# A language-model tower: routing with unrolled loops, 64-column blocks and filler passes, and a table with picks in pairs

## The chip, the cores and the metric

One core of a Trainium2 chip runs the kernel. The metric is the device time of one execution in microseconds (us), the median of several runs; before the change it is 1200.1 us (three runs, 1199.15 to 1202.99). Engines: TensorE (PE; its weight loads PEld), VectorE (DVE), ScalarE (ACT), GpSimd (POOL) and SyncE (SP), each with its own stream of instructions, ordered between engines by semaphores alone.

## The reference

64 batches of 128 tokens, width 192. Three steps, each added to the residual h:

```
h = layernorm(concat(word_emb[x] + pos_emb, three graph features) @ W_proj.T + b_proj)
h = h + (causal long convolution per channel of layernorm(h)) + bias * layernorm(h)
x = layernorm(h)
top2, idx = top_k(x @ Wr.T, 2)           # 8 experts
w = softmax(top2)
h = h + sum over the two picks of w * (gelu(x @ Wi[e].T + bi[e]) @ Wo[e].T + bo[e])
```

The expert step computes only the picked experts: tokens are sorted by expert into tiles of 256 slots.

## The kernel before

The stages follow one another in time on the one core.

*Tokens* (0 to 491 us): gathers, graph features, projection and normalisation, in rounds of one quad (Q = 4 batches of 128 rows). *Convolution* (491 to 539 us): fp32 matmuls of 128 columns (L614), the results added to `Hs` by VectorE.

*Routing* (539 to 625 us), the stage that most of the change touches. Sixteen quads, in four groups g of four (GRP = 16 batches). For quad i, with p = i mod 2:

- VectorE: statistics of the rows of a group (L1032) and from these scale and shift (`scales`, L1034: a chain of small instructions). Before the first quad it does those of quads 0 and 1, 2 and 3, and group 1; those of groups 2 and 3 follow between the rankings of groups 0 and 1 (`groups`, L1089).
- ScalarE, `row_parts` (L826): four instructions (L830) write the normalised rows to `xn[p]`, fp32, 192 wide; one more (L834) rounds them to bf16 into the row table `xrow` (`hi`).
- GpSimd, `low` (L482): copies the last 64 columns of each row side by side into `xn1` (L486), waits for `hi_done`, and subtracts the rounded from the full values (L489, L490), the `lo` part.
- TensorE, `turn_quad` (L628): four transposes of the first 128 columns into bank 1 (L633), two of `xn1` into bank 2 (L635). It waits for `ln_done`, `xn1_ready` and `xnT_ready`.
- ScalarE, `turned_parts` (L836): two copies from PSUM to `xnT0` and `xnT1` (L839, L840).
- TensorE, `score` (L638): the fp32 product with the router's weights, six matmuls, which run as two passes each, of 16 columns (L643) and 8 (L645), into one of the four banks 3 to 6; it waits until the quad four back has been ranked (`gap_ready`).
- VectorE, `choices` (L1042): the two largest of eight scores and their places (L1047 to L1051).
- A group behind, the softmax of two (`gap_exp`, `shares`) and the one-hot counts (`rank`, L648: two bf16 products).

TensorE's order is: transposes of quad i+1, scores of quad i (`routes`, L659). ScalarE's: rows of quad i+1, copies of quad i. `steps` (L79) runs the first and the last rounds written out and those between in a loop of the engine. SyncE stores `Hs` and `xrow` by groups (`store_rows`, L401) once a group's weights are there, then loads the first experts' weights (L428, L431).

*Table* (625 to 670 us): VectorE turns counts into slots (L1116 to L1144). Then TG = 16 steps, double-buffered: VectorE compares slot numbers with a ramp, 142 values by eight picks for `hot_q` and 128 by eight for `hot_p` (`one_hot`, L1147); ScalarE scales `hot_q` into `hot_s`, four picks an instruction (L872); TensorE sums eight products `hot_p` x `hot_s`, each of 142 columns, in banks 5 and 6 (L680). The picks are innermost, so that the matmul of pick i reads both operands at a step of eight bf16 values, 16 bytes. Behind step 1 VectorE works out the expert of each tile (`experts`, L1151).

*Identifiers* (670 to 680 us): small VectorE instructions, then gathers of the first rows by GpSimd (L501), transposes by TensorE (L694). *Experts* (680 us to the end): 71 tiles, TensorE nearly throughout.

## Time and profile before

| what | value |
|---|---|
| median of three runs | 1200.1 us |
| profiled execution | 1199.93 us, span of its instructions 1198.0 us |
| mean granted clock of TensorE | 0.784 of 2.4 GHz |
| busy: TensorE / VectorE / ScalarE / GpSimd | 955.7 / 615.1 / 518.6 / 670.7 us |

The busy share of TensorE is 80%, but it is a mean over stages with different limits, and it counts a matmul at 1.2 GHz for twice what it would take at 2.4. So the page is read by stage: windows of the trace give each engine's busy time and the granted clock in a stretch, the timeline gives the distance from start to start of the same instruction in neighbouring quads or steps, which is what a quad or step costs. The times of engines other than TensorE don't hang on the granted clock.

### The profile page before, as it was taken

How to read it: one execution, taken by the hardware profiler on the slowest of the kernel's cores; microseconds unless marked ns; L12 is line 12 of the kernel's file. 1: busy time of each engine (PE TensorE's matmuls, PEld its weight loads, DVE VectorE, ACT ScalarE, POOL GpSimd, SP SyncE). 2: the span in 40 equal slices, each digit the busy share in tenths (PEclk: the TensorE clock that was granted, in tenths of full speed). 3: DMA queues.
4: the chain of work that ended last, by engine and by line, in shares of the span. 5: the costliest groups of instructions: out<-in, count | busy, mean ns of one | idle time of the engine just before them, and what ended most of it. 6: DMA issues, size and time to landing. Idle time of an engine off the chain costs nothing. (4 is left out here: it accounts for less than half of the span.)

```text
span 1198.0 us, 22895 instructions
## 1 busy us (share of the span) xinstructions
PE 955.7 (80%) x7666; PEld 907.0 (76%) x7666; DVE 615.1 (51%) x2089; ACT 518.6 (43%) x1211; POOL 670.7 (56%) x592
## 2 busy tenths in 40 slices
PE   1678677768677687594977699999988998999991
PEld 0578677778677687594964399999978998999981
DVE  2035343445444456538957356665544654665551
ACT  1002121311212123355755376767655665767660
POOL 6455564646565640003520268867767777888774
PEclk9975665656665666795555599999999999999996
DMA  6315261616162533581098174485486465434342
GB/s 208 106 53 176 81 209 53 217 50 214 46 222 94 170 110 114 167 241 53 1 256 263 28 199 62 61 224 129 86 218 151 60 141 120 61 61 61 61 51 30
DMA packets 101114, 146.96 MB, mean 123 GB/s; under 512 B 13476, under 2 KB 81223, under 8 KB 98983
## 3 DMA queue, kind: packets, MB, share of 16 engines
q0 software_dynamic: 39552, 53.26, 23.0%
q1 hardware_dynamic: 60470, 82.26, 21.8%
q10 hardware_dynamic: 1008, 10.34, 2.4%
q8 instruction: 50, 0.82, 0.3%
q14 instruction: 34, 0.27, 0.1%
HBM read 107.00 MB, written 38.82 MB: 122 GB/s over the span
## 5 line engine op out<-in xcount | busy, mean ns | idle before, releaser
L883 ACT ACTIVATE Hs<-bank,U 128x256 bf16<-128x256 f32 x426 | 212.4, 498 | 182.6 <-PE bank L715 153.8
L474 POOL DMA_INDIRECT ev_g<-in_word_emb,ids_i x192 | 192.9, 1004 | 166.1 <-PE bank L573 111.9
L510 POOL DMA_INDIRECT out<-Hs,id_s x142 | 236.6, 1666 | 85.4 <-issue 83.3
L1204 DVE TENSOR_TENSOR Hs<-Hs 128x512 bf16<-128x512 f32 x213 | 147.5, 692 | 146.6 <-ACT Hs L884 131.3
L884 ACT ACTIVATE Hs<-bank,U 128x256 f32<-128x256 f32 x426 | 214.6, 504 | 0.0
L730 PE MATMUL bank<-U,Hs 128*128 128x192 bf16 x852 | 211.6, 248 | 0.2 <-issue 0.2
L732 PE MATMUL bank<-U,Hs 128*128 128x192 bf16 x852 | 209.9, 246 | 0.0
L731 PE MATMUL bank<-U,Hs 128*128 128x192 bf16 x852 | 209.7, 246 | 0.0
L501 POOL DMA_INDIRECT blob<-xtab_d,id_g x142 | 144.2, 1015 | 111.7 <-DVEq L1188 61.1
L573 PE MATMUL bank<-cs,ev_g 128*128 128x1 f32 x384 | 97.8, 318 | 42.6 <-issue 42.6
L572 PE MATMUL bank<-cs,ev_g 128*128 128x1 f32 x384 | 96.1, 314 | 39.4 <-issue 39.3
L572 PEld LDWEIGHTS bank<-cs,ev_g 128*128 128x128 f32 x384 | 93.4, 293 | 39.7 <-issue 39.5
L573 PEld LDWEIGHTS bank<-cs,ev_g 128*128 128x128 f32 x384 | 94.8, 298 | 37.5 <-issue 37.5
L711 PE MATMUL bank<-blob,U 128*128 128x256 bf16 x426 | 116.7, 274 | 2.1 <-DVE blob L1193 2.1
L712 PE MATMUL bank<-blob,U 128*128 128x256 bf16 x426 | 116.6, 274 | 0.0
L713 PE MATMUL bank<-blob,U 128*128 128x256 bf16 x426 | 116.6, 274 | 0.0
L714 PE MATMUL bank<-blob,U 128*128 128x256 bf16 x426 | 116.6, 274 | 0.0
L715 PE MATMUL bank<-blob,U 128*128 128x256 bf16 x426 | 116.6, 274 | 0.0
L731 PEld LDWEIGHTS bank<-U,Hs 128*128 128x128 bf16 x852 | 84.2, 99 | 0.1
L730 PEld LDWEIGHTS bank<-U,Hs 128*128 128x128 bf16 x852 | 83.2, 98 | 0.5 <-issue 0.4
L732 PEld LDWEIGHTS bank<-U,Hs 128*128 128x128 bf16 x852 | 83.0, 97 | 0.1
L469 POOL DMA_INDIRECT emb_g<-in_word_emb,ids_i x64 | 61.7, 963 | 26.7 <-issue 18.6
(183 smaller groups left out, 1735.2 us busy)
## 6 DMA issues: line engine op xcount, KB each, us to landing
U<-blob_d SPq DMA_DIRECT2D x20, 771.0 KB
U<-blob_d SPq DMA_DIRECT2D x20, 672.0 KB
adj_s<-in_adj SPq DMA_DIRECT2D x48, 256.0 KB
ev_g<-kpad_d SPq DMA_DIRECT2D x24, 512.0 KB, 5.3
wst<-in_wsrc SPq DMA_DIRECT2D x8, 1344.0 KB
blob_d<-blob ACTq DMA_DIRECT2D x7, 1443.0 KB
xtab_d<-U SPq DMA_DIRECT2D x4, 1552.0 KB, 8.8
out<-Hs SPq DMA_DIRECT2D x4, 1536.0 KB, 11.5
```

Source lines behind the costliest of these rows:

```text
L474: pool.indirect_dma_start(ev_g[:, p, j, b, :], None, t["word_emb"], bass.IndirectOffsetOnAxis(ap=ids_i[:, 1 + j, i * Q + b:i * Q + b + 1], ...
L501: pool.indirect_dma_start(xg_f[:, q % RX, h, :], None, xtab_d, bass.IndirectOffsetOnAxis(ap=id_g[:, 2 * q + h:2 * q + h + 1], axis=0)).the ...
L510: pool.indirect_dma_start(out, bass.IndirectOffsetOnAxis(ap=id_s[:, 2 * q + h:2 * q + h + 1], axis=0), yo[:, q % RX, h, :], None, compute_ ...
L572: mm(bank[3][:, k:k + 1], ev_g[:, p, j, b, 0:D0], cs[:, p, k:k + 1], start=True, stop=True)
L573: last = mm(bank[3][:, 16 + k:17 + k], ev_g[:, p, j, b, D - 128:D], cs[:, p, k:k + 1], start=True, stop=True)
L711: mm(ps, hi[:, a], x0, start=True, stop=False)
L730: mm(ps, hh[w][:, f, n], hi[:, c], start=f == 0, stop=False)
L731: mm(ps, hh[w][:, f, n], lo[:, c], start=False, stop=False)
L732: last = mm(ps, hl[w][:, f, n], hi[:, c], start=False, stop=f == FC - 1)
L883: f(hh[w][:, d, :], ps, ACT.Gelu, bias=bi[:, d:d + 1])
L884: last = f(hf[w][:, d, :], ps, ACT.Gelu, bias=bi[:, d:d + 1])
L1204: last = v.tensor_tensor(hl[w][:, c:c + 2, :], hf[w][:, c:c + 2, :], hh[w][:, c:c + 2, :], ALU.subtract)
```

## The change

- Routing: the loops of TensorE, ScalarE, VectorE and GpSimd are written out.
- The normalised rows go into three blocks of 64 columns, each block with the quad's four batches side by side (`xn[p, r, b, d]`). A transpose takes two neighbouring batches of one block; so `xn1` and its copy are gone. The router's weights lie block-diagonal for every block (`wr`, loaded by two DMAs instead of three), and all twelve score passes have 16 columns. Scores go to three banks (LB = 3) instead of four.
- The bf16 rounding of a quad is done by GpSimd, ahead of its subtractions, instead of by ScalarE.
- TensorE gets filler passes, bf16 matmuls of 256 columns whose result nobody reads: 56 ahead of the first transposes, 3 behind each quad's transposes, 4 behind each quad's scores, 45 ahead of the table and 40 behind it.
- Table: the tiles have two picks innermost, `[a, m, n, i]` with i of 2, so that a matmul reads at a step of two values, 4 bytes. `iota_r` shrinks with it, and ScalarE's two instructions a step read and write without gaps.

```diff
@@ -36,6 +36,9 @@
 TG = 16
 TB = B // TG
 PICKS = 2 * TB
+XR = D // D1
+LB = 3
+FILL_LN, FILL_TURN, FILL_SCORE, FILL_SLOTS, FILL_IDS = 56, 3, 4, 45, 40
 ID_0 = float((127 + 7 - B) * S)
 NFFT = 2 * S
 EPS_TOK, EPS_LN = 1e-12, 1e-5
@@ -105,7 +108,7 @@
         ones_b = sb("ones_b", [128, 128], bf16)
         zero_f = sb("zero_f", [128, 2, D])
         iota_f = sb("iota_f", [128, 256])
-        iota_r = sb("iota_r", [128, NC, PICKS], bf16)
+        iota_r = sb("iota_r", [128, NC, 2], bf16)
 
         cst = sb("cst", [128, 128 + 128 + 256 + 128 + 1 + NC + 2 * TG])
         powers = cst[:, 641 + NC:641 + NC + 2 * TG].rearrange("p (k g) -> p k g", k=2)
@@ -185,7 +185,7 @@
             assert at[0] <= 2 * GRAPHS * Q * D
             return rt[:, at[0] - n:at[0]]
 
-        xn = carve(2 * Q * D).rearrange("p (a q d) -> p a q d", a=2, q=Q)
+        xn = carve(2 * Q * D).rearrange("p (a r q d) -> p a r q d", a=2, r=XR, q=Q)
 
         oh = [carve(E * B).rearrange("p (e b) -> p e b", e=E) for _ in range(2)]
         sl = carve(E * B).rearrange("p (e b) -> p e b", e=E)
@@ -480,20 +478,22 @@
 
 
             def low(i, p):
+                b = bass.ds(i * Q, Q)
+                by_row = xn[:, p, :, :, :].rearrange("p r b d -> p b r d")
+                hi = xrow[:, b, 0:D].rearrange("p b (r d) -> p b r d", r=XR)
+                lo = xrow[:, b, D + D1:2 * D].rearrange("p b (r d) -> p b r d", r=XR - 1)
                 pool.wait_ge(ln_done, i + 1)
-                after(pool, xn_t, i - 1)
-                pool.sem_inc(pool_turn, 1)
-                nc.gpsimd.tensor_copy(xn1[:, p, :].rearrange("p (b d) -> p b d", b=Q), xn[:, p, :, D0:D]).then_inc(xn1_ready, 1)
+                nc.gpsimd.tensor_copy(hi, by_row).then_inc(hi_done, 1)
                 pool.wait_ge(hi_done, i + 1)
-                b = bass.ds(i * Q, Q)
-                nc.gpsimd.tensor_tensor(xrow[:, b, D:D + D1], xn[:, p, :, D0:D], xrow[:, b, D0:D], ALU.subtract)
-                nc.gpsimd.tensor_tensor(xrow[:, b, D + D1:2 * D], xn[:, p, :, 0:D0], xrow[:, b, 0:D0], ALU.subtract).then_inc(lo_done, 1)
+                nc.gpsimd.tensor_tensor(xrow[:, b, D:D + D1], xn[:, p, XR - 1, :, :], xrow[:, b, D0:D], ALU.subtract)
+                nc.gpsimd.tensor_tensor(lo, by_row[:, :, 0:XR - 1, :], hi[:, :, 0:XR - 1, :], ALU.subtract).then_inc(lo_done, 1)
 
             def lows(it):
                 for p in range(2):
                     low(2 * it + p, p)
 
-            steps(pool, NQ // 2, lows)
+            for it in range(NQ // 2):
+                lows(it)
 
             def fetch(q):
                 after(pool, hid, q - RX + 1)
@@ -625,25 +625,32 @@
                     chunk(it, s)
 
 
+            def filler(n, room):
+
+                for _ in range(n):
+                    mm(room[:, 0:256], identb[:, :], repeat(tri[:, :], 1, 2), start=True, stop=True)
+
             def turn_quad(i, p):
                 pe.wait_ge(ln_done, i + 1)
-                pe.wait_ge(xn1_ready, i + 1)
                 after(pe, xnT_ready, i)
-                for b in range(Q):
-                    nc.tensor.transpose(bank[1][:, b * 128:(b + 1) * 128], xn[:, p, b, 0:D0], ident[:, :])
-                for h in range(Q // 2):
-                    last = nc.tensor.transpose(bank[2][:, h * 128:(h + 1) * 128], xn1[:, p, h * 128:(h + 1) * 128], ident[:, :])
+                for r in range(XR):
+                    for h in range(Q // 2):
+                        n = ((2 * r + h) % 4) * 128
+                        pair = xn[:, p, r, 2 * h:2 * h + 2, :].rearrange("p b d -> p (b d)")
+                        last = nc.tensor.transpose(bank[1 + r // 2][:, n:n + 128], pair, ident[:, :])
                 last.then_inc(xn_t, 1)
+                filler(FILL_TURN, bank[6])
 
             def score(i, s):
                 p = s % 2
                 pe.wait_ge(xnT_ready, i + 1)
-                after(pe, gap_ready, i - QG + 1)
+                after(pe, gap_ready, i - LB + 1)
                 for h in range(Q // 2):
-                    mm(bank[3 + s][:, h * 2 * E:(h + 1) * 2 * E], xnT1[:, p, h * 128:(h + 1) * 128], wr1, start=True, stop=False)
-                    for b in (2 * h, 2 * h + 1):
-                        last = mm(bank[3 + s][:, b * E:(b + 1) * E], xnT0[:, p, b * 128:(b + 1) * 128], wr0, start=False, stop=b % 2 == 1)
+                    for r in range(XR):
+                        last = mm(bank[3 + i % LB][:, h * 2 * E:(h + 1) * 2 * E], xnT[:, p, 2 * r + h, :],
+                                  wr[:, r, :, :].rearrange("p h e -> p (h e)"), start=r == 0, stop=r == XR - 1)
                 last.then_inc(logits, 1)
+                filler(FILL_SCORE, bank[6])
 
             def rank(g):
 
@@ -653,8 +660,6 @@
                     to_g = bank[to][:, :].rearrange("p (e b) -> p e b", e=E)[:, :, bass.ds(g * GRP, GRP)]
                     last = mm(to_g, w[:, :], hot, start=True, stop=True)
                 last.then_inc(ranks, 1)
-
-            turn_quad(0, 0)
 
             def routes(g):
                 for s in range(QG):
@@ -665,8 +670,12 @@
                     if s == QG - 1 and not (isinstance(g, int) and g == 0):
                         rank(g - 1)
 
-            steps(pe, NG, routes, last=1)
+            filler(FILL_LN, bank[1])
+            turn_quad(0, 0)
+            for g in range(NG):
+                routes(g)
             rank(NG - 1)
+            filler(FILL_SLOTS, bank[6])
 
 
             zero_b = zero_f[:, 0, 0:64].bitcast(bf16)
@@ -677,11 +686,12 @@
                 pe.wait_ge(hot_p_ready, g + 1)
                 pe.wait_ge(hot_s_ready, g + 1)
                 for i in range(PICKS):
-                    last = mm(sums(i % TB), hot_p[:, g % 2, :, i], hot_s[:, g % 2, :, i], start=False, stop=False)
+                    last = mm(sums(i % TB), hot_p[:, g % 2, i // 2, :, i % 2], hot_s[:, g % 2, i // 2, :, i % 2], start=False, stop=False)
                 last.then_inc(pick_used, 1)
             for x in (5, 6):
                 last = mm(bank[x][:, 0:2 * NC], zero_b, ramp, start=False, stop=True)
             last.then_inc(table, 1)
+            filler(FILL_IDS, bank[4])
             pe.wait_ge(ids_done, 1)
 
             xT_ps = bank[0][:, :].bitcast(bf16)
@@ -827,17 +837,15 @@
                 after(act, xn_t, i - 1)
                 after(act, lo_done, i - 1)
                 for b in range(Q):
-                    last = f(xn[:, p, b, :], Hs[:, bass.ds(i * Q + b, 1), :].rearrange("p b d -> p (b d)"), ACT.Identity,
+                    last = f(xn[:, p, :, b, :], Hs[:, bass.ds(i * Q + b, 1), :].rearrange("p b (r d) -> p (b r) d", r=XR), ACT.Identity,
                              scale=ln3[:, 0, bass.ds(i * Q + b, 1)], bias=ln3[:, 1, bass.ds(i * Q + b, 1)])
                 last.then_inc(ln_done, 1)
-                act.wait_ge(ln_done, i + 1)
-                f(xrow[:, bass.ds(i * Q, Q), 0:D], xn[:, p, :, :], ACT.Copy).then_inc(hi_done, 1)
 
             def turned_parts(i, p):
                 act.wait_ge(xn_t, i + 1)
                 after(act, logits, i - 1)
-                f(xnT0[:, p, :], bank[1][:, :], ACT.Copy)
-                f(xnT1[:, p, :], bank[2][:, 0:2 * 128], ACT.Copy).then_inc(xnT_ready, 1)
+                f(xnT[:, p, 0:4, :], bank[1][:, :].rearrange("p (c n) -> p c n", c=4), ACT.Copy)
+                f(xnT[:, p, 4:6, :], bank[2][:, 0:256].rearrange("p (c n) -> p c n", c=2), ACT.Copy).then_inc(xnT_ready, 1)
 
             def gap_exp(g):
                 act.wait_ge(gap_ready, QG * (g + 1))
@@ -868,8 +877,8 @@
                 act.wait_ge(hot_q_ready, g + 1)
                 after(act, pick_used, g - 1)
                 for k in range(2):
-                    i = slice(k * TB, (k + 1) * TB)
-                    last = f(hot_s[:, g % 2, :, i], hot_q[:, g % 2, :, i], ACT.Copy, scale=powers[:, k, g:g + 1])
+                    m = slice(k * TB // 2, (k + 1) * TB // 2)
+                    last = f(hot_s[:, g % 2, m, :, :], hot_q[:, g % 2, m, :, :], ACT.Copy, scale=powers[:, k, g:g + 1])
                 last.then_inc(hot_s_ready, 1)
             act.wait_ge(h_out, 16 * (NG + 1))
 
@@ -1042,7 +1051,7 @@
             def choices(i, s):
 
                 dve.wait_ge(logits, i + 1)
-                lg = bank[3 + s][:, 0:Q * E].rearrange("p (b e) -> p b e", b=Q)
+                lg = bank[3 + i % LB][:, 0:Q * E].rearrange("p (b e) -> p b e", b=Q)
                 for b in range(Q):
                     v.max(top[:, s % 2, b, :], lg[:, b, :])
                 fence()
@@ -1145,8 +1155,8 @@
             fence()
 
             def one_hot(out, places, g, width):
-                here = places[:, g, :, :].rearrange("p k t -> p (k t)")
-                return v.tensor_tensor(out, iota_r[:, 0:width, :], repeat(here, 1, width), ALU.is_equal)
+                here = places[:, g, :, :].rearrange("p k (m i) -> p (k m) i", i=2)
+                return v.tensor_tensor(out, repeat(iota_r[:, 0:width, :], 1, PICKS // 2), repeat(here, 2, width), ALU.is_equal)
 
             def experts():
 
@@ -1159,9 +1169,9 @@
 
             for g in range(TG):
                 after(dve, hot_s_ready, g - 1)
-                one_hot(hot_q[:, g % 2, :, :], slq, g, NC).then_inc(hot_q_ready, 1)
+                one_hot(hot_q[:, g % 2, :, :, :], slq, g, NC).then_inc(hot_q_ready, 1)
                 after(dve, pick_used, g - 1)
-                one_hot(hot_p[:, g % 2, :, :], slp, g, 128).then_inc(hot_p_ready, 1)
+                one_hot(hot_p[:, g % 2, :, :, :], slp, g, 128).then_inc(hot_p_ready, 1)
                 if g == 1:
                     experts()
 
```

## Rows read from the trace of the kernel before

**Rows 1.** Windows: stretch, length, each engine's busy us (count), clock, DMA, GB/s.
```profile
565.00:582.00 17.00, 14.35 (x71) 14.29 (x70) 15.40 (x98) 13.49 (x28) 8.78 (x12) 0.50 0.01 2
634.00:670.00 36.00, 33.07 (x128) 18.43 (x129) 23.50 (x37) 22.82 (x32) 0.00 (x0) 0.50 0.53 176
680.00:700.00 20.00, 17.92 (x170) 15.55 (x169) 9.12 (x21) 12.30 (x33) 10.34 (x11) 0.88 0.44 124
```

**Rows 2.** Timeline of TensorE in routing: start, us, engine, line, what [idle before].
```profile
568.97 1.09 PE L633 MATMUL bank<-ident,ev_g 128*128 128x128 f32 x4 [2.65 <-ACT adj_s L840]
...
576.42 1.09 PE L633 MATMUL bank<-ident,ev_g 128*128 128x128 f32 x4
...
577.74 0.45 PE L643 MATMUL bank<-wr,adj_s 128*128 128x16 f32 x2
...
580.16 1.09 PE L633 MATMUL bank<-ident,ev_g 128*128 128x128 f32 x4
...
619.94 1.00 PE L645 MATMUL bank<-wr,adj_s 128*128 128x8 f32 x4
```

**Rows 3.** Timeline of ScalarE over one quad in routing.
```profile
572.19 1.85 ACT L830 ACTIVATE ev_g<-Hs,ln 128x192 f32 x4
...
574.18 0.84 ACT L834 ACTIVATE U<-ev_g 128x768 f32 x1
...
575.67 1.85 ACT L830 ACTIVATE ev_g<-Hs,ln 128x192 f32 x4
```

**Rows 4.** Waits from 545 to 634 us: who, for whom, us, times, longest.
```profile
DVE top L1047 <- PE bank L645: 9.9, 5, 3.2
```

**Rows 5.** Timeline of the table stage.
```profile
634.57 0.75 DVE L1149 TENSOR_TENSOR adj_s<-iota_r,slq 128x1136 bf16<-128x1136 bf16 x1
...
635.35 2.75 ACT L872 ACTIVATE adj_s<-adj_s,cst 128x568 bf16<-128x568 bf16 x4 [11.40 <-DVE adj_s L1149]
...
635.84 0.74 DVE L1149 TENSOR_TENSOR adj_s<-iota_r,slq 128x1136 bf16<-128x1136 bf16 x1
...
636.89 3.00 PEld L680 LDWEIGHTS bank<-adj_s,wst 128*128 128x128 bf16 x13 [11.53 <-DVE wst L1149]
...
639.75 12.44 PE L680 MATMUL bank<-adj_s,wst 128*128 128x142 bf16 x47
```

**Rows 6.** Groups of GpSimd's instructions in routing: busy, mean ns | idle before.
```profile
L490 POOL TENSOR_TENSOR U<-ev_g,U 128x512 f32 (+1 forms) x16 | 18.6, 1160 | 0.0
...
L489 POOL TENSOR_TENSOR U<-ev_g,U 128x256 f32 (+1 forms) x16 | 10.9, 682 | 9.1 <-ACT U L834 9.1
...
L486 POOL COPY adj_s<-ev_g 128x256 f32<-128x256 f32 x16 | 6.4, 398 | 122.4 <-ACT ev_g L830 121.7 <-PE bank L635 0.7
```

**Rows 7.** Timeline where GpSimd and VectorE meet.
```profile
575.93 1.16 POOL L490 TENSOR_TENSOR U<-ev_g,U 128x512 f32 x1
...
576.08 1.04 DVE L967 SCALAR_TENSOR_TENSOR rs<-rs 128x16 f32<-128x16 f32 x1
```

**Rows 8.** Timeline of TensorE: convolution's end, experts' start.
```profile
535.76 2.57 PE L614 MATMUL bank<-U,adj_s 128*128 x22
...
683.39 0.42 PE L712 MATMUL bank<-blob,U 128*128 128x256 bf16 x1
...
683.60 0.42 PE L713 MATMUL bank<-blob,U 128*128 128x256 bf16 x1
```

**Rows 9.** Windows around a rise and a fall of the clock.
```profile
492.00:496.00 4.00, 4.00 (x20) 4.00 (x21) 1.04 (x2) 0.50 (x1) 0.00 (x0) 0.50 0.70 277
...
496.00:500.00 4.00, 4.00 (x34) 4.00 (x34) 1.03 (x3) 1.62 (x2) 0.00 (x0) 0.89 0.98 257
...
540.00:544.00 4.00, 0.00 (x0) 0.00 (x0) 3.55 (x22) 0.00 (x0) 0.00 (x0) 0.66 0.89 282
```

**Rows 10.** Timeline: SyncE's first expert load, TensorE's first expert transposes.
```profile
643.07 0.39 SPq L428 DMA_DIRECT2D U<-blob_d  x1
...
679.61 0.80 PE L694 MATMUL bank<-identb,blob 128*128 128x128 bf16 x6 [8.82 <-DMA blob<-xtab_d,id_g]
```

29 lines of the change are left out of this document (13 added, 16 removed).

## The prediction

> **What bounds the kernel now.** I read the mean clock per stretch first, then the order of instructions of one quad (four batches, the unit of the routing stage), then the table loop. The kernel is a chain of stages, so a gain counts only in the stage where it falls. Tokens (0 to 491 us) and experts (680 us on) are not touched. The change lies between 538 and 680 us: the routing stage, then the table that sorts picks into slots, then the identifiers. In all of it TensorE runs at 0.50 of its clock, 1.2 GHz, against 0.88 in the 20 us after [rows 1].
>
> In the routing stage each quad is normalised by ScalarE, transposed by TensorE, copied back by ScalarE, scored by TensorE and ranked by VectorE. Where nothing stands in the way, the three engines are close. TensorE needs 1.32 us for six transposes (576.42 to 577.74) and 2.42 us for twelve score passes (to 580.16), 3.74 us a quad, without a pause [rows 2]. ScalarE needs 3.48 us (572.19 to 575.67), of which the bf16 copy at line 834 is 0.84 us [rows 3]. VectorE sits at 15.4 us busy of 17 in the first two groups [rows 1]; it waits for the scores only 9.9 us in all, in five places [rows 4]. So VectorE sets the pace up to about 600 us, and TensorE with ScalarE after that.
>
> The table loop is TensorE's: six steps of eight matmuls take 12.44 us, 2.07 us a step; ScalarE does four of its halves in 2.75 us, so a step's two in about 1.37 us; VectorE's two comparisons take 1.27 us (634.57 to 635.84) [rows 5].
>
> **The change, part by part.**
>
> *bf16 copy to GpSimd.* ScalarE loses 0.84 us a quad, and would need about 2.6 us. GpSimd loses its 0.40 us copy of 256 columns and gains one of 768. Bounds from the nearest rows: 0.8 us (the subtractions cost 682 ns for 256 and 1160 ns for 512 columns, some 1.9 ns a column with two inputs, and I halve it for one, with 0.2 fixed) and 1.2 us (three copies of 398 ns) [rows 6]. I take 1.0. With the subtractions, which overlap a little, GpSimd needs about 3.05 us a quad. That is less than a quad takes in every case below but the warm one. TensorE no longer waits for GpSimd before a transpose.
>
> *GpSimd against VectorE.* A small VectorE instruction that meets a GpSimd one stands: the update at 576.08 takes 1.04 us against 0.17 for its like, and ends with the subtraction that began at 575.93 [rows 7]. GpSimd is busy 8.8 of 17 us now [rows 1] and more with the wider copy, which comes at once behind the normalisation, so the chain of small instructions that ends in the scales is interrupted a few times more. I charge 1.5 us once to the time at which the scales of the second group are ready; the bounds are 0 and 3 (three more such stops). The Trainium skill's "SBUF — State Buffer", section "SBUF: two separate sides", has a GpSimd instruction that reads SBUF and a VectorE one with two SBUF inputs exclude each other for the whole instruction; the trace agrees, and by that rule every wider copy can stop VectorE once for up to 1.0 us, 8 us over the two groups in which VectorE sets the pace, against the 1.5 us taken here.
>
> *Blocks of 64 columns.* Six transposes and six fp32 products (twelve passes) a quad remain; a score pass of 8 columns costs what one of 16 does, since passes lie 0.21 us apart in either [rows 2]. Nothing is gained or lost. Three score banks instead of four make a score wait for the ranking three quads back; VectorE is less than that behind when TensorE sets the pace. Nothing, at most 1 us.
>
> *Loops unrolled.* The stage has one or two loop rounds an engine, and TensorE shows no pause in them; nothing, with 1 us either way.
>
> *Fillers in the routing.* Seven passes of 256 columns a quad, three behind the transposes and four behind the scores, in TensorE's order ahead of the next quad's work. At 1.2 GHz such passes lie 0.21 us apart (683.39 to 683.60); at 2.4 GHz 22 passes that take as many cycles each are done in 2.57 us, 0.11 us apart when the last one's own length is left out [rows 8]. So a quad costs 3.74 + 7 x 0.213 = 5.23 us cold, and warm about 3.74/2 + 7 x 0.11 = 2.6 us. Everything hangs on which it is.
>
> *Is the clock raised?* The rows show what went before a rise and a fall. It rose between 496 and 500 us, after fp32 matmuls of 128 columns without a pause from 492; it fell between 540 and 544, TensorE having been idle from 538.3 [rows 8, 9]. It never rose from 548 to 670, though TensorE was busy 14.4 of 17 us and 33.1 of 36 in it [rows 1]: passes of 8 or 16 columns behind fp32 weights, and the table's strided ones, do not raise it. The new mix is 0.85 (filler) + 1.32 (transposes) + 0.64 (filler) = 2.8 us of wide passes and then 2.4 us of narrow ones. That is between the two. And the 56 fillers at the head (6 us at the full clock, from 538.3) can't carry the clock over: the transposes come at 548, and the second and third groups of scales leave TensorE idle for some 5 us and again for some (the transposes at 568.97 stood 2.65 us [rows 2]); when its own passes are twice as fast the holes are wider. So I expect it to fall by about 558; the rise in the rows came behind an unbroken run of wide passes, and cold routing has none. I take cold. The Trainium skill's "TensorE: Matmul & The Clock Gate", Part 4, says that the full clock does not engage for transposes, which do not count as busy in the same way; by it only the fillers would count here and the warm case below would go. No row here shows transposes alone.
>
> Cold, then: from the transposes at 568.97 to the end of the last score at 620.9 [rows 2] TensorE now takes 51.9 us for twelve transposed quads and thirteen scores; its own work is 12 x 3.74 + 2.42 + 0.6 (three small rank products) = 47.9 us. With fillers it is 47.9 + 12 x 0.64 + 12 x 0.85 = 65.8 us, and now nothing else is late enough to stop it (VectorE, busy 15.4 of 17 us over four quads in the first groups, needs about 4 us a quad there). The start moves by +1.5 - 0.84. Routing: 65.8 - 51.9 + 0.7 = **+14.5 us** (12 to 17).
>
> *Table.* With the two picks innermost, matmul operands are read at a step of 4 bytes, not 16. The rows have no such step: the upper bound is 0.26 us a pass (2.07/8), the lower 142 columns at 1.2 GHz, 0.12 us, as the 256-column passes do it in 0.21 [rows 5, 8]. I take 0.12 since those are the nearest in packing; then TensorE needs 1 us a step and ScalarE is last with 1.37, rather 1.38 to 1.45 with its waits. The three extra VectorE instructions behind step 1, hidden by TensorE now, come into sight, so that step 2 starts no earlier than it does. The other fourteen steps gain 14 x (2.07 - 1.38) = **-9.7 us** (-6 to -10.5; 0 if the operands' pace does not change). The 45 fillers before it need 9.6 us cold; TensorE stands 11.53 us there [rows 5]: free. If that cover were short by n passes, 0.2 us each.
>
> *Fillers over the identifiers.* 40 passes, 8.5 us cold, in a hole of which the last 8.8 us are put down to the gathers [rows 10]: free, with 1 us at risk. If the clock is then up when the experts start, up to 2.4 us come back (0.12 of 20 us lost there now, at half speed [rows 1]); they end some 3 us ahead of the first expert pass, so I take 0 (0 to -2.4).
>
> *Transfers.* The first expert's weights are issued at 643.07, once the routed rows are stored, 36 us ahead of the experts' first transposes at 679.61 [rows 10]. Cold routing moves the stores by 14.5 us and the transposes by 4.8, which leaves 27 us. Hidden.
>
> Sum: the profiled execution took 1199.9 us (span 1198.0), 0.2 under the median of 1200.1. 1199.9 + 14.5 - 9.7 = **1204.7 us**, with its own range of 1199 to 1210.
>
> **The rivals.**
>
> *A. Warm (the other side: faster).* Fillers and wide transposes hold 2.4 GHz through most of the routing, from group 1 on at least. TensorE's quad is 2.6 us and drops off the path; VectorE's pace holds to 600 us, plus 1.5, and then GpSimd's 3.05 us a quad. Last four quads: 4 x (3.74 - 3.05) = 2.8 us; drain at twice the clock, (1.32 + 2 x 2.42)/2 = 3.1; -0.84 +1.5: -5.2 us. With the table -9.7 and the head of the experts -2.4: 1182.6 us. It decides once a rise survives the waits for scales. For it: more than half of a quad's TensorE time would be wide passes, which no part of the stage has now. Against: the pauses above.
>
> *B. Between.* The clock comes and goes by quads. Halfway in the routing, +4.6, -9.7, -1.2: 1193.7 us.
>
> *C. VectorE's comparison loses its pace.* It writes 2160 values in 1.27 us, about two a cycle; with an innermost run of two values it might do one, 2.4 us a step [rows 5]. The table would take 40 us against 35: +4.5 in place of -9.7, with cold routing 1219 us. The Trainium skill's "Vector Engine (DVE) Microarchitecture Reference", section 5.1, asks for step 1 and 16-bit values and more than one value innermost; by that the pace is kept.
>
> *D. The table keeps TensorE's pace*, the step being no help: 1214 us with cold routing.
>
> **How the numbers follow.** Cold 0.52, warm 0.20, between 0.19, C 0.04, D 0.05. The range takes in the cold case with its bounds, B and A: 1181 to 1210. A measurement can tell some 0.3% (3.6 us) from no change. Faster: A, most of B and a little of cold, 0.39. Same: two fifths of cold and a little of B, 0.24. Slower: 0.37.
>
> **What would show it.** Granted clock of the routing stretch: 0.5 and a spacing of 5.2 us between quads' transposes for the forecast, 1.0 and about 3 to 4 us for A. Table: ScalarE's pairs back to back at 1.4 us a step, TensorE idle between steps; spacing 2.07 would be D, VectorE comparisons of 1.2 us C. GpSimd copy near 1.0 us. It is wrong if a mixed run of wide and narrow passes suffices to raise or hold the clock.

## The result, and the profile after

The changed kernel takes 1195.2 us, the kernel before, run beside it, 1201.8 us (medians of 20 runs each). The ratio is 0.9949 with a 95% interval of 0.9929 to 0.9969: 0.5% faster, 3.7 to 8.5 us. The profiled execution took 1194.4 us (span 1192.4), against 1199.9 (1198.0) before. Its mean granted clock is 0.815 against 0.784. The time before the first statistics of the rows (VectorE; counted from the small memsets in front of them) scatters by execution, so the two traces are compared by stages:

| stage | before | after | difference |
|---|---|---|---|
| up to the first statistics | 539.30 | 541.85 | +2.55 |
| routing: first statistics to last index | 82.89 | 84.65 | +1.76 |
| last index to the table's first comparison | 12.38 | 12.43 | +0.05 |
| table: first comparison to the read of its sums | 36.26 | 26.22 | -10.04 |
| identifiers: to the experts' first transposes | 8.78 | 8.92 | +0.14 |
| experts | 518.40 | 518.31 | -0.09 |

The sum is -5.63 us. The first line belongs to no part of the change. So the change is worth 8.2 us here: the table gives 10.0, the routing takes 1.8 back.

**Routing.** Windows of the changed kernel (columns as in [rows 1]):

```profile
561.00:573.00 12.00, 12.00 (x59) 11.05 (x60) 10.71 (x64) 6.94 (x17) 7.02 (x9) 0.50 0.00 0
573.00:577.00 4.00, 4.00 (x38) 3.93 (x36) 3.85 (x32) 3.53 (x9) 3.84 (x5) 0.95 0.02 4
577.00:583.00 6.00, 1.79 (x17) 1.44 (x16) 5.06 (x14) 2.30 (x6) 3.80 (x5) 1.00 0.00 1
583.00:588.00 5.00, 3.59 (x18) 3.44 (x19) 4.63 (x47) 1.97 (x5) 0.57 (x1) 0.57 0.00 0
590.00:597.00 7.00, 7.00 (x65) 6.83 (x66) 6.47 (x41) 6.11 (x15) 4.37 (x7) 0.97 0.01 4
597.00:603.00 6.00, 1.38 (x13) 1.04 (x10) 5.32 (x21) 1.89 (x5) 3.59 (x4) 0.81 0.00 0
603.00:614.00 11.00, 10.76 (x53) 10.04 (x53) 6.05 (x62) 5.30 (x13) 5.66 (x6) 0.50 0.71 185
615.00:625.00 10.00, 10.00 (x97) 9.73 (x97) 7.78 (x61) 5.34 (x14) 5.39 (x6) 1.00 0.74 218
```

The clock column (the third from the right) is to be read beside TensorE's time, the first after the length. A stretch is called cold at 0.50 (1.2 GHz) and warm at 1.00 (2.4 GHz). TensorE is busy all 12 us from 561, at 0.50; then the clock is up (573). TensorE now outruns VectorE and idles (1.79 of 6), and from 583 it is cold again. That happens twice, and the last stretch is warm to its end. Before, the clock stood at 0.50 from 541.3 us, 2 us into the routing, to its end. TensorE's timeline shows what a quad costs at either clock:

```profile
566.07 1.49 PE L640 MATMUL bank<-ident,ev_g 128*128 128x128 f32 x6
567.35 0.85 PE L631 MATMUL bank<-tri,identb 128*128 128x256 bf16 x3
567.99 2.58 PE L650 MATMUL bank<-wr,adj_s 128*128 128x16 f32 x12
570.41 1.01 PE L631 MATMUL bank<-tri,identb 128*128 128x256 bf16 x4
571.22 1.49 PE L640 MATMUL bank<-ident,ev_g 128*128 128x128 f32 x6
...
574.97 0.82 PE L640 MATMUL bank<-ident,ev_g 128*128 128x128 f32 x6
...
577.64 0.60 PE L640 MATMUL bank<-ident,ev_g 128*128 128x128 f32 x4
...
584.41 1.86 PE L650 MATMUL bank<-wr,adj_s 128*128 128x16 f32 x8 [5.62 <-DVE topi L1060]
```

A cold quad is 571.22 - 566.07 = 5.15 us, a warm one 2.67. The hole before 584.41 is TensorE waiting for the ranking (L1060) that frees one of three score banks. The waits in routing:

```profile
DVE top L1056 <- PE bank L650: 7.4, 5, 3.1
...
ACT wsm L852 <- DVE topi L1060: 15.0, 3, 6.0
...
PE bank L650 <- DVE topi L1060: 10.5, 2, 5.6
```

VectorE waits 7.4 us for scores, 9.9 before [rows 4]. Take these from the stage and VectorE's own time is left: 82.89 - 9.9 = 73.0 us before, 84.65 - 7.4 = 77.3 after. The waits fell by 2.5 us and VectorE's own time rose by 4.3. The 2.5 us can't be put down to the clock alone: the kernel without quad fillers (below) is cold throughout and waits only 6.7 us, with VectorE still later.

Where VectorE lost its time is read from its small instructions, by group. Changed kernel:

```profile
L966 DVE TENSOR_SCALAR rs<-rs 128x16 int32<-128x16 int32 (+1 forms) x5 | 3.5, 695 | 0.4
...
L974 DVE TENSOR_TENSOR rs<-rs 128x16 f32<-128x16 f32 (+1 forms) x15 | 5.0, 331 | 1.1
```

the same two groups, kernel before:

```profile
L957 DVE TENSOR_SCALAR rs<-rs 128x16 int32<-128x16 int32 (+1 forms) x5 | 1.9, 382 | 0.4
...
L965 DVE TENSOR_TENSOR rs<-rs 128x16 f32<-128x16 f32 (+1 forms) x15 | 4.2, 283 | 1.1
```

Both belong to the chain that ends in the scales. All its lines together (L955 to L967 before, L964 to L976 after) add up to 17.9 us before and 22.5 after; the ranking's (L1047 to L1051, L1056 to L1060) to 25.1 and 24.8. So in this execution nearly the whole loss lies in the chain, and most of it in the two chains that run between the rankings: 4.5 us each before, 5.8 for the third group and 7.2 for the fourth after. In the fourth group's chain, instructions that take 0.17 to 0.21 us alone stand one after the other beside GpSimd's, and end with them:

```profile
596.22 0.68 DVE L974 TENSOR_TENSOR rs<-rs 128x16 f32<-128x16 f32 x1
596.97 1.05 DVE L976 SCALAR_TENSOR_TENSOR rs<-rs 128x16 f32<-128x16 f32 x1
598.09 0.84 DVE L972 TENSOR_TENSOR rs<-rs 128x16 f32<-128x16 f32 x1
...
596.19 0.67 POOL L488 TENSOR_TENSOR U<-ev_g,U 128x256 bf16<-128x256 f32 x1
596.82 1.17 POOL L489 TENSOR_TENSOR U<-ev_g,U 128x512 bf16<-128x512 f32 x1
598.08 0.82 POOL L486 CAST U<-ev_g 128x768 bf16<-128x768 f32 x1
```

GpSimd's copy by group, now at 0.85 us:

```profile
L486 POOL CAST U<-ev_g 128x768 bf16<-128x768 f32 x16 | 13.6, 849 | 128.9 <-ACT ev_g L840 128.9
```

**Table.** Timeline of the changed kernel (answers to [rows 5]):

```profile
638.93 0.75 DVE L1159 TENSOR_TENSOR adj_s<-iota_r,slq 128x1136 bf16<-128x1136 bf16 x1
...
652.40 0.85 PEld L689 LDWEIGHTS bank<-adj_s,wst 128*128 128x128 bf16 x8 [0.48 <-issue]
652.43 1.10 PE L689 MATMUL bank<-adj_s,wst 128*128 128x142 bf16 x8 [0.22 <-ACT adj_s L881]
...
653.88 1.10 PE L689 MATMUL bank<-adj_s,wst 128*128 128x142 bf16 x8 [0.34 <-ACT adj_s L881]
...
655.21 1.11 PE L689 MATMUL bank<-adj_s,wst 128*128 128x142 bf16 x8 [0.23 <-ACT adj_s L881]
```

Two steps take 655.21 - 652.43 = 2.78 us, 1.39 each, where one took 2.07. TensorE does its eight matmuls in 1.10 us and waits for ScalarE in front of every step. The comparison still takes 0.75 us.

**Behind the table** nothing came forward:

```profile
664.91 4.86 PE L631 MATMUL bank<-tri,identb 128*128 128x256 bf16 x40
...
674.07 0.80 PE L704 MATMUL bank<-identb,blob 128*128 128x128 bf16 x6 [4.30 <-DMA blob<-xtab_d,id_g]
```

The fillers end 4.3 us ahead of the gathered rows, and the experts' transposes are cold as before [rows 10].

### The profile page after: what moved, and what is told of

It reads as the page before. It is cut to its first block and busy times, and to the rows that moved or that the text cites. A ratio compares the mean times of both kernels' runs of the same rounds, so it can differ in the third digit from the quotient of the medians.

```text
span 1192.4 us, 23175 instructions
## 1 busy us (share of the span) xinstructions
PE 952.0 (80%) x7919; PEld 907.5 (76%) x7919; DVE 617.9 (52%) x2089; ACT 505.5 (42%) x1195; POOL 677.4 (57%) x592
## 3 DMA queue, kind: packets, MB, share of 16 engines
q1 hardware_dynamic: 60582, 82.26, 22.5%
## 5 line engine op out<-in xcount | busy, mean ns | idle before, releaser
L501 POOL DMA_INDIRECT blob<-xtab_d,id_g x142 | 146.0, 1028 | 98.5 <-DVEq L1198 47.8
L572 PE MATMUL bank<-cs,ev_g 128*128 128x1 f32 x384 | 94.6, 310 | 45.6 <-issue 45.4
L573 PE MATMUL bank<-cs,ev_g 128*128 128x1 f32 x384 | 96.0, 313 | 42.1 <-issue 42.1
L572 PEld LDWEIGHTS bank<-cs,ev_g 128*128 128x128 f32 x384 | 91.8, 288 | 44.2 <-issue 44.1
L573 PEld LDWEIGHTS bank<-cs,ev_g 128*128 128x128 f32 x384 | 92.9, 292 | 37.8 <-issue 37.8
L486 POOL CAST U<-ev_g 128x768 bf16<-128x768 f32 x16 | 13.6, 849 | 128.9 <-ACT ev_g L840 128.9
L741 PEld LDWEIGHTS bank<-U,Hs 128*128 128x128 bf16 x852 | 84.3, 99 | 0.1
```

Of the source, the lines that this page charges most:

```text
L501: pool.indirect_dma_start(xg_f[:, q % RX, h, :], None, xtab_d, bass.IndirectOffsetOnAxis(ap=id_g[:, 2 * q + h:2 * q + h + 1], axis=0)).the ...
L572: mm(bank[3][:, k:k + 1], ev_g[:, p, j, b, 0:D0], cs[:, p, k:k + 1], start=True, stop=True)
L573: last = mm(bank[3][:, 16 + k:17 + k], ev_g[:, p, j, b, D - 128:D], cs[:, p, k:k + 1], start=True, stop=True)
L741: mm(ps, hh[w][:, f, n], lo[:, c], start=False, stop=False)
```

## Experiments

Every kernel's routing is read in the same way: its length from the first statistics to the last index, VectorE's waits for scores in it, and what is left, VectorE's own time; each from one profile. "Ratio" is to the kernel before, run beside it, with its 95% interval. In eight of the runs the whole program was some 100 us shorter, the kernel before too (medians of 1098.1 and 1100.7 us): their token stage ended at some 440 us instead of 540, so the windows below lie earlier. Why is not known.

| kernel | routing | waits | own | ratio |
|---|---|---|---|---|
| before | 82.89 | 9.9 | 73.0 | |
| changed | 84.65 | 7.4 | 77.3 | 0.9949 (0.9929 to 0.9969) |
| table layout only | 82.89 | 9.9 | 73.0 | 0.9919 (0.9888 to 0.9949) |
| routing only | 92.27 | 15.0 | 77.3 | 0.9974 (0.9941 to 1.0007) |
| no quad fillers | 85.71 | 6.7 | 79.0 | 0.9949 (0.9926 to 0.9972) |
| no fillers | 85.70 | 6.7 | 79.0 | 0.9931 (0.9906 to 0.9957) |
| ... four banks | 83.07 | 5.3 | 77.8 | 0.9938 (0.9904 to 0.9971) |
| ... copy on ScalarE | 82.79 | 8.7 | 74.1 | 0.9953 (0.9914 to 0.9991) |
| ... both | 82.66 | 9.0 | 73.7 | 0.9968 (0.9925 to 1.0011) |
| transposes as fillers | 84.75 | 7.6 | 77.2 | 1.0012 (0.9962 to 1.0062) |
| fillers, four banks | 82.85 | 5.5 | 77.4 | 0.9933 (0.9903 to 0.9963) |
| the same, copy on ScalarE | 79.17 | 3.9 | 75.3 | 0.9959 (0.9927 to 0.9991) |
| the same, 14 fillers | 79.85 | 4.7 | 75.2 | 0.9959 (0.9932 to 0.9985) |
| changed, second time | 79.34 | 1.8 | 77.5 | 0.9960 (0.9935 to 0.9986) |
| changed, third | 84.83 | 6.5 | 78.3 | |
| changed, fourth | 88.32 | 10.9 | 77.4 | |
| three fillers | 88.62 | 12.2 | 76.4 | |
| fillers in the quads only | 81.25 | 7.0 | 74.3 | 0.9873 (0.9824 to 0.9922) |

"..." are variants of the one without quad fillers. The ratios carry the scatter of the token stage, and most overlap; mechanisms are read from the stages. But the changed kernel alone gave 79.3 to 88.3 us of routing in four executions, so a few us between two kernels whose clock comes and goes decide nothing. Where it stays down (no quad fillers) two profiles agree within 0.01 us.

**Table layout alone**, the kernel before with

```diff
-        iota_r = sb("iota_r", [128, NC, PICKS], bf16)
+        iota_r = sb("iota_r", [128, NC, 2], bf16)
...
-                    last = mm(sums(i % TB), hot_p[:, g % 2, :, i], hot_s[:, g % 2, :, i], start=False, stop=False)
+                    last = mm(sums(i % TB), hot_p[:, g % 2, i // 2, :, i % 2], hot_s[:, g % 2, i // 2, :, i % 2], start=False, stop=False)
```

> The kernel before with the new layout of the table tiles (two picks innermost) and nothing else. Theory: the whole gain of the change is the table's, so this kernel is about 10 us faster than before (ratio 0.992), that is as fast as the changed kernel or some 2 us faster, its table stage takes 26 us instead of 36, ScalarE's slices stand back to back at 1.38 us a step and TensorE idles between steps at 0.50 of its clock. Rival (the table's gain needs the fillers or is partly taken back behind it): less than 7 us, or a table stage over 29 us.

Its table stage took 26.49 us, 9.8 less than before. Its window, all of that stage:

```profile
533.30:559.70 26.40, 18.16 (x130) 13.76 (x130) 22.76 (x35) 22.12 (x32) 0.00 (x0) 0.50 0.67 229
```

ScalarE is busy 22.1 of 26.4 us, TensorE 18.2, at half its clock. The table's gain is whole without any filler or block.

**The rest of the change alone**, the changed kernel with the old table layout:

```diff
-        iota_r = sb("iota_r", [128, NC, 2], bf16)
+        iota_r = sb("iota_r", [128, NC, PICKS], bf16)
```

> The changed kernel with the old table layout: 64-column blocks, bf16 copy on GpSimd, three score banks, unrolled loops and all fillers. Theory (the clock's gain and the fillers' own time cancel in the routing): 0 to +4 us against before (ratio 1.000 to 1.003), the clock rises about 573 and falls in two holes behind VectorE. Rival 1 (the fillers do pay): -2 us or less. Rival 2 (the forecast's cold routing, which this one trace happened to miss): +10 us or more.

Its profiled execution took 1112.9 us against a median of 1095.7, so it is one execution's course and not the kernel's rule. The clock was up twice, and then:

```profile
506.00:532.00 26.00, 26.00 (x129) 24.07 (x129) 12.38 (x105) 11.30 (x28) 10.94 (x12) 0.50 0.75 227
...
DVE top L1056 <- PE bank L650: 15.0, 6, 3.9
```

26 us on end at 0.50 with TensorE never idle, in the last five quads, where VectorE has no statistics left to do and TensorE sets the pace. VectorE's own time is 77.3 us as in the changed kernel; the waits have doubled. Seven fillers a quad are thus no warrant for a rise. In the median the kernel is 2.9 us under before (-6.5 to +0.8), which shuts out the cold routing of the forecast and leaves the other two open.

**Without quad fillers, and without any:**

```diff
-FILL_LN, FILL_TURN, FILL_SCORE, FILL_SLOTS, FILL_IDS = 56, 3, 4, 45, 40
+FILL_LN, FILL_TURN, FILL_SCORE, FILL_SLOTS, FILL_IDS = 56, 0, 0, 45, 40
```

> The changed kernel without the seven fillers of every quad; those at the head, before the table and over the identifiers stay. Theory (gain and cost cancel): the clock stays at 0.50 from 550 us to the end of the routing, a quad takes 3.7 us on TensorE, and the time is within 2 us of the changed kernel. Rival 1 (fillers pay): 3 us or more slower than the changed kernel, VectorE waiting over 12 us for scores. Rival 2 (fillers cost): 3 us or more faster, since the ScalarE relief then counts without a tax.

> The changed kernel with no filler anywhere. Theory: the fillers at the head, before the table and over the identifiers stand in holes and save nothing behind them, so this is within 1 us of the kernel without quad fillers; the first transposes are then cold. Rival: the head's fillers save some of the first quad (up to 1.9 us) or those over the identifiers some of the experts' head (up to 2.4 us), and it is slower by that.

Without quad fillers the clock stays down, in a stretch without a pause too:

```profile
502.00:521.00 19.00, 19.00 (x94) 19.00 (x94) 12.32 (x86) 9.46 (x23) 9.47 (x11) 0.50 0.95 284
...
PE bank L650 <- DVE topi L1060: 6.8, 2, 4.4
```

The routing took 85.7 us in both, 2.8 more than before though neither pays for a filler in a quad, and about as much as with them. So the fillers about cancel, and something else costs 2.8 us. With all fillers gone (56, 45 and 40 to zero too) no stage became longer: those at the head, before the table and over the identifiers bring nothing.

**Which part costs the 2.8 us:** the kernel without quad fillers, with four banks; with the copy back on ScalarE; with both.

```diff
-LB = 3
+LB = 4
...
-                nc.gpsimd.tensor_copy(hi, by_row).then_inc(hi_done, 1)
...
                 last.then_inc(ln_done, 1)
+                act.wait_ge(ln_done, i + 1)
+                f(xrow[:, bass.ds(i * Q, Q), 0:D].rearrange("p b (r d) -> p b r d", r=XR), xn[:, p, :, :, :].rearrange("p r b d -> p b r d"), ACT.Copy).then_inc(hi_done, 1)
```

> The kernel without quad fillers (its routing took 85.7 us from the first statistics to the last index, against 82.9 before) with four score banks again. Theory (GpSimd's wider copy delays VectorE, the third bank is nearly free): 85.7 us, at most 0.5 us less. Rival (the third bank costs): 84 us or less, and TensorE waits less than 2 us for VectorE's indices where it waited 6.8 us.

> The kernel without quad fillers, with the bf16 copy on ScalarE again and no copy at all on GpSimd. Theory (GpSimd against VectorE): VectorE's own instructions from the first statistics to the first comparison lose the 5 to 6 us that they gained against before (98.7 us before, 105.1 without fillers), and the routing comes to 82.5 to 83.5 us although ScalarE has 0.84 us a quad more. Rival (ScalarE's relief was worth something, contention is small): 86 to 88 us.

> The kernel without quad fillers, with four score banks and with the copy on ScalarE. What is left of the change in the routing is the 64-column blocks and the unrolled loops. Theory: as before or a little under it, 82 to 83 us, since no copy runs on GpSimd at all. Rival (the blocks or the unrolled code cost something of their own): 84 us or more.

Taking the copy off GpSimd gives VectorE back 4.9 us with three banks and 4.1 with four. The fourth bank gives the routing 2.6 us with the copy on GpSimd and 0.1 without. I had expected nothing from it: wrong. The two parts cost together what neither costs alone: with four banks the copy costs VectorE 4.1 us of its own time, but the routing only 0.4 (83.07 against 82.66), since the waits shrink from 9.0 to 5.3 us. GpSimd makes VectorE late; with four banks TensorE runs ahead meanwhile and the lateness is taken out of VectorE's later waits; with three it stops. TensorE's wait for the ranking in the kernel with four banks:

```profile
PE bank L650 <- DVE topi L1060: 1.6, 2, 0.9
```

**Do transposes count?** The changed kernel with

```diff
+            def turn_filler(n, room):
+                for _ in range(n):
+                    nc.tensor.transpose(room[:, 0:128], ident[:, :], ident[:, :])
...
-                filler(FILL_TURN, bank[6])
+                turn_filler(FILL_TURN, bank[6])
```

behind the transposes, and the same behind the scores.

> The changed kernel with the seven fillers of a quad made fp32 transposes of 128 columns, which take as long (1.32 us for six). The head's, the table's and the identifiers' fillers are as they were. Theory (any long enough pass raises the clock, in a mixed run too): the granted clock in the routing still comes and goes between 0.50 and 1.00, and the routing takes 84 to 93 us. Rival (transposes do not count): 0.50 from some 10 us after the first statistics to the end of the routing, 5.2 us a quad on TensorE throughout, routing 94 us or more.

```profile
568.23 0.84 PE L636 MATMUL bank<-ident 128*128 128x128 f32 x3
...
567.00:579.00 12.00, 12.00 (x58) 12.00 (x59) 10.71 (x64) 6.78 (x17) 7.02 (x9) 0.50 0.00 0
579.00:589.00 10.00, 5.91 (x53) 5.67 (x51) 8.95 (x45) 6.03 (x14) 7.74 (x9) 0.98 0.01 2
```

Three transposes take the 0.84 us that three fillers took (0.85), and the clock comes up in the same place, and three times in the routing, as in the changed kernel: the routing is 84.75 us. Beside the narrow scores and the small rank products TensorE had nothing but transposes here, and with the six transposes of a quad alone the clock had stayed down (above). The rule that they do not count, which I had cited against the warm case (the Trainium skill, "TensorE: Matmul & The Clock Gate", Part 4), does not hold for these fp32 ones. Its ratio, 1.0012, touches the changed kernel's only at the edge of the intervals. Its profiled span is 7.8 us longer than that of the changed kernel, 6.0 of it ahead of the routing and 1.8 in the experts, neither of which was touched; why stays open.

**Fewer fillers:** three a quad.

```diff
-FILL_LN, FILL_TURN, FILL_SCORE, FILL_SLOTS, FILL_IDS = 56, 3, 4, 45, 40
+FILL_LN, FILL_TURN, FILL_SCORE, FILL_SLOTS, FILL_IDS = 56, 3, 0, 45, 40
```

> The changed kernel with three fillers a quad, behind the transposes, and none behind the scores. Theory (what stands between the narrow score passes has to be a large part of the run): the clock stays at 0.50 in the routing, a cold quad takes 3.74 + 0.64 = 4.4 us on TensorE, VectorE waits over 8 us for scores, routing 87 to 89 us. Rival (any filler will do): the clock rises in the routing at least once.

```profile
508.00:530.00 22.00, 22.00 (x108) 21.03 (x108) 9.16 (x77) 8.34 (x20) 8.97 (x10) 0.50 0.89 265
```

The clock did not rise in the routing. VectorE's waits came to 12.2 us: this is the pure cost, 88.6 us against 85.7 without quad fillers. Three buy nothing. Over all runs: once it had fallen at the head, the clock never rose in the routing in the eight profiles with no or three fillers a quad, and rose at least twice in each of the ten with seven or more.

**The holes:** four banks, the seven fillers ahead of the scores in the bank that these then fill; then the copy on ScalarE and 64 fillers over the identifiers; then 14 fillers in the quads 2 to 11. With the banks the fillers' place changes too: none stands behind the transposes or the scores any more.

```diff
-                pe.wait_ge(xnT_ready, i + 1)
                 after(pe, gap_ready, i - LB + 1)
+                filler(7, bank[3 + i % LB])
...
+                filler(14 if 2 <= i < 12 else 7, bank[3 + i % LB])
...
+                pe.wait_ge(xnT_ready, i + 1)
```

> The changed kernel with four score banks; the seven fillers of a quad stand together ahead of its scores, in the bank that the scores then use, since no other bank is free. Copy on GpSimd. Theory (the clock falls in the holes in which TensorE waits for VectorE, and the third bank makes those holes): fewer or shorter holes (under 4 us of waiting for indices against 10.5), the clock up for more than the 34 of 84 us of the changed kernel, routing 82 to 84 us. Rival (the holes are VectorE's own and come with any number of banks, or the phase of the clock's rises decides): the clock comes and goes as before and the routing takes 85 to 93 us.

> As the kernel with fillers and four banks, with the bf16 copy on ScalarE again, so that VectorE has its undisturbed pace, and 64 fillers over the identifiers instead of 40, to reach the first rows. Theory: VectorE waits 9.9 us for scores in the routing of before; where the clock is up these waits go, so the routing takes 76 to 80 us. Rival 1 (fillers cost while the clock is down what they give while it is up): 83 to 86 us. For the identifiers: theory, the experts' passes start at the full clock, so that the sixtieth up pass ends 9.2 us after the first transpose instead of 11.6 to 11.9; rival, the fillers run late and the first transpose comes later than 8.8 us after the table.

> As the one above with 14 fillers instead of 7 for the quads 2 to 11, those in which VectorE sets the pace. At the full clock a quad then takes 2.67 + 0.75 = 3.4 us on TensorE, still under VectorE's 4 and more; at half of it 6.7 us. Theory (the clock is held where TensorE has no hole of several us): up through the quads 2 to 11 once risen, VectorE waits under 5 us for scores, routing 76 to 79 us. Rival (the cold stretch ahead of the rise costs more than the rise returns): routing over 84 us.

With four banks the wait for the ranking fell from 10.5 to 1.9 us, as expected. But the clock, from its first fall on, was up for only 27 us of the routing, against 33 in the changed kernel: fewer holes did not keep it up. It stayed down through an almost unbroken stretch first:

```profile
563.00:594.00 31.00, 30.00 (x145) 27.42 (x145) 28.19 (x183) 18.05 (x44) 18.18 (x21) 0.50 0.00 1
```

So the theory of the holes holds for the waits and not for the clock. The routing, 82.85 us, met its 82 to 84, but lies within what the changed kernel gives by itself. With the copy on ScalarE it is 79.2 us, as expected, and here the clock fell at 590.6 although TensorE had not stood for more than 0.83 us at once since the rise at 576.9. Where the clock was up, ScalarE set the pace in this kernel, with 3.38 us a quad against the 2.67 of a warm quad of the changed kernel:

```profile
615.25 0.85 PE L639 MATMUL bank<-ident,ev_g 128*128 128x128 f32 x6 [0.40 <-ACT adj_s L848]
...
618.63 0.85 PE L639 MATMUL bank<-ident,ev_g 128*128 128x128 f32 x6 [0.52 <-ACT adj_s L848]
```

Doubling the fillers raised the time at full clock from 37.5 to 47.8 us and the routing was 79.9, 0.9 above the range expected: nothing gained. The added time lies where VectorE sets the pace, or ScalarE.

The longer fill over the identifiers failed by another way than its rival. The clock was up at the first transposes, and they were not late (8.84 us behind the table), but the sixtieth pass of the experts began 15.2 us after them instead of 11.6 to 11.9 (the expectations say "ends"; the figures are those of its start).

**The changed kernel again**, unchanged, three times.

> The changed kernel once more, for a second profile of it. Its routing took 84.7 us in the first; the same routing with the old table took 92.3, the clock having been down for 27 us on end. Theory (the clock's rises and falls hang on where in time the unbroken stretches lie, which differs by execution): any value from 84 to 93 us. Rival (the pattern of rise and fall is fixed by the instructions): 84.7 us within 0.5 and the same places of rise and fall.

> The changed kernel a third time. Theory: the routing is VectorE's own 77.3 us plus its waits for scores (7.4, 15.0 and 1.8 us so far), and the waits are set by when the clock is up: between 79 and 93 us. Rival (one value is the rule, the others are accidents): 84.7 within 0.5.

> The changed kernel a fourth time, expectations as for the third: VectorE's own time 77.3 us within 0.3 whatever the clock does, and a routing of 79 to 93 us; by the rival 84.7 within 0.5.

The second time:

```profile
588.00:605.00 17.00, 16.35 (x81) 15.19 (x81) 15.43 (x114) 8.15 (x20) 7.86 (x9) 0.51 0.01 2
605.00:625.00 20.00, 19.76 (x184) 19.07 (x183) 16.80 (x126) 14.00 (x34) 13.14 (x15) 0.99 0.79 239
...
DVE top L1056 <- PE bank L650: 1.8, 3, 0.8
```

Here the clock was up for the last 20 us, and the waits came to 1.8 us. From its first fall on it was up for 30 us, less than the 33 of the first profile, and yet the routing was 5.3 us shorter: where the rise lies counts, and not its share. Four profiles of the same instructions gave 84.65, 79.34, 84.83 and 88.32 us, with VectorE's own time at 77.3 to 78.3. The second fell below the 84 to 93 us expected of it; the rival of one fixed value met the third profile, and fell with the second and the fourth. VectorE was busy 69.4 us of the routing in the first and in the second, against 64.8 before, but not in the same place: in the second the chain of the scales took 18.9 us, and the one-hot comparisons (L1083) 4.1 where they had taken 1.9 before (L1074). The mean, 84.3, is 1.4 above before. This and the table's 10.0 would make 8.6 us; the ratio says 3.7 to 8.5.

The same execution shows ScalarE's first two pairs of GELU in the experts:

```profile
676.48 0.47 ACT L892 ACTIVATE Hs<-bank,U 128x256 bf16<-128x256 f32 x1 [14.16 <-issue]
...
680.12 0.47 ACT L892 ACTIVATE Hs<-bank,U 128x256 bf16<-128x256 f32 x1 [2.07 <-PE bank L725]
```

The second pair stood 2.07 us, where the changed kernel's first profile has 0.21. The sixtieth pass then began 14.9 us after the first transposes. This happened in 4 of 12 profiles with 40 fillers over the identifiers, in both with 64, and in none of the four without. In all six the clock was up at the experts' first transposes; it was in three of the other twelve too, and there the pair was not late. So fillers here carry this risk, but what holds the pair up was not found.

**Fillers where they may pay, and nowhere else:** four banks, copy on ScalarE, seven fillers a quad (their number stands in the call), and the three other counts at zero. Against the kernel with four banks and the copy on ScalarE:

```diff
-FILL_LN, FILL_TURN, FILL_SCORE, FILL_SLOTS, FILL_IDS = 56, 3, 4, 45, 64
+FILL_LN, FILL_TURN, FILL_SCORE, FILL_SLOTS, FILL_IDS = 0, 3, 4, 0, 0
```

> Four score banks, seven fillers a quad in the bank of the scores, copy on ScalarE, and no fillers at the head, before the table or over the identifiers. Theory: VectorE's own time is 75.2 us, waits 2 to 8 us, so routing 77 to 83 us; the experts' sixtieth pass ends 11.6 to 11.9 us after the first transpose; against before 10 to 14 us faster, ratio 0.990. Rival (the fillers over the identifiers have nothing to do with the experts' late start): the sixtieth pass ends at 14.9 us here too, and the ratio stays at 0.995.

```profile
482.00:502.00 20.00, 16.37 (x145) 15.39 (x144) 17.86 (x115) 16.46 (x35) 9.31 (x11) 0.99 0.01 2
502.00:516.00 14.00, 12.34 (x61) 11.02 (x61) 9.45 (x88) 10.88 (x24) 5.47 (x6) 0.53 0.73 219
516.00:526.00 10.00, 9.09 (x84) 8.69 (x82) 6.25 (x57) 3.92 (x9) 1.84 (x2) 0.98 0.91 274
```

Routing 81.25 us, table 26.2, the sixtieth pass at 11.3. The ratio is 0.9873 (0.9824 to 0.9922), 14 us under before (8.6 to 19.4). The two stages give 11.7 of them. That it beats the changed kernel is not shown, though its interval lies under the other's: the two executions of the changed kernel run beside it took 1087.3 and 1090.8 us, and its own six 1080.1 to 1091.4, with a median of 1086.2. Against the table layout alone the intervals overlap. In the one profile the clock was still down from 502 to 516. A kernel with fillers in the last quads alone, which TensorE paces, was not run.

## Why the prediction was wrong

The forecast was 1204.7 us, 4.8 slower; the profiled execution took 1194.4, and the kernel is faster. The case called "between" (1193.7) names the mechanism that happened, the clock coming and going; that its figure lies within 0.7 us is luck. Its +4.6 us in the routing came out at +1.8 in this profile (-3.6 to +5.4 in four), its -1.2 at the experts' head did not come, and 2.55 us of the measured time are scatter ahead of the routing.

- **The step that failed: "Is the clock raised?", taken as cold.** It rested on this: the rise in the rows came behind an unbroken run of wide passes, "and cold routing has none". The routing has unbroken stretches (12 us from 561), they need not be wide throughout, and the clock rose behind them. What the forecast named as its refutation, "a mixed run of wide and narrow passes suffices", is what happened in all ten profiles with seven or more fillers a quad (transposes in one); with three it did not. It suffices sometimes and not always: such runs stood at 0.50 for 26 and 30 us. The rule on transposes that I set beside this step spoke for the wrong side.
- **The cost of a quad was right**: 5.23 us cold and 2.6 warm in the forecast, 5.15 and 2.67 in the trace. The first fall was forecast by about 558 us and came at 549.5. Whether +14.5 us was the right price of a cold routing no run shows, since none with seven fillers was cold throughout; the one that was down for its last 26 us came to 92.3 us, +9.4 in all, and the cold one with three fillers to 88.6, where the same reckoning gave 87 to 89.
- **GpSimd against VectorE was mis-sized**: 1.5 us charged, with 3 at most, for the scales of the second group. The place named was right in kind, the chain of small instructions that ends in the scales; but the second group's scales came only some 0.4 us later, and 4 us were lost in the chains of the third and fourth. VectorE's own time grew by 4.3 us; taking the copy off GpSimd gives back 4.1 to 4.9. The rule of the Trainium skill's "SBUF — State Buffer", section "SBUF: two separate sides", gave up to 8 us; the measured loss lies between.
- **Three banks, "Nothing, at most 1 us", failed**: 2.6 us with the copy on GpSimd, and with the fillers 10.5 us in which TensorE waits for the ranking. "VectorE is less than that behind when TensorE sets the pace" holds only for the last five quads; in the others VectorE sets it.
- **ScalarE's relief** was priced at -0.84 once. While the clock is down it is worth nothing: the copy going back to ScalarE made nothing longer. Where the clock is up ScalarE with the copy needs 3.38 us a quad and TensorE waits for it, so there the relief is worth up to 0.7 us a quad, which no part of the forecast has.
- **Copy on GpSimd**: 1.0 us forecast, 0.85 measured. Two of its sums don't come out: the lower bound by its own rows is 0.72 + 0.2 = 0.92 us, not 0.8, and GpSimd's terms are 1.0 + 0.68 + 1.16 = 2.84 us a quad, not 3.05. Neither changes the forecast; the second would make rival A some 0.8 us faster. Unrolled loops and blocks: 82.66 against 82.89 us with copy, banks and quad fillers undone, nothing, as forecast.
- **Table: right.** -9.7 forecast, -10.0 measured, by the mechanism named: ScalarE last, 1.38 a step against 1.39, TensorE at 0.12 us a pass. Rivals C and D fell: the comparison is still 0.75 us.
- **Identifiers**: 0 forecast, +0.14 measured. The 1 us set at risk did not come in this profile; in others 3 us came by a way that I had not seen, in the experts' second pair of GELU.

So what the clock gave in the routing went into three places: the fillers' own time while the clock is down, VectorE's 4.3 us, and TensorE's waits for the ranking, in which a full clock is of no use. How the gain divides among them differs by execution.

## What to carry over

Split a stage into the time of the engine that paces it and that engine's waits; what is done to another engine can return the waits at most (9.9 us here), and only where they lie. What slows the pacing engine can be taken out of its waits, as long as the others run ahead meanwhile: with four banks the copy cost VectorE 4.1 us and the routing 0.4, with three 4.9 and 2.9. So moving work to an engine beside which the pacing one's instructions stand still, and taking a buffer away behind it, should be priced together. Filler passes pay only if the clock rises behind them, and this differs by execution; here no kernel with them was shown to beat the new table layout alone.

## What the runs showed of the hardware

- Granted clock: down through 19 us (no quad fillers) and 22 us (three a quad) of TensorE without a pause; up behind stretches of the same kind with seven 256-column passes, or seven fp32 transposes, a quad, but not each time (30 of 31 us busy at 0.50). It fell behind holes of some 5 us, and once where TensorE had not stood for more than 0.83 us at once. The same instructions met it in different places in different executions, 79 to 88 us for one stage.
- A matmul of 142 bf16 columns read at a step of 16 bytes takes 0.26 us at half the clock, at 4 bytes 0.12. VectorE's comparison does not care whether two or eight values are innermost (0.75 us for 1136 values).
- A 0.17 us VectorE instruction takes up to 1.05 us beside a GpSimd one; a GpSimd conversion of 768 columns from fp32 to bf16 takes 0.85 us.
- In six profiles ScalarE's second pair of GELU began about 2 us late though TensorE had delivered. All six had fillers over the identifiers. What holds it up was not found.
